# Cross-attention: the last quarter of V's projection as three products of parts, and a ring of nine probability tiles

## What is computed

```
q = x @ w_q                                   # 512 x 320
k = text @ w_k;  v = text @ w_v               # 1593 x 320, contraction over 512
out_text = softmax(q k^T / 4) v               # per head
out_ip   = softmax(q k_ip^T / 4 + mask) v_ip  # per head, 8 tokens, mask from boxes
y = (out_text + out_ip) @ w_out + b_out + x
```

## Time and profile before

| | |
|---|---|
| median of three runs | 1859.44 us (1856.71 to 1864.67) |
| profiled execution | 1859.6 us |
| its span | 1857.8 us, 42311 instructions |
| TensorE busy | 98% of the span |
| VectorE, ScalarE, GpSimd busy | 72%, 64%, 20% |
| chain that ended last | TensorE 94%, VectorE 4%, DMA 1%, issue 1% |
| mean granted TensorE clock | 0.992 |

### The profile page before, as it was taken

The page is one execution under the profiler, slowest core; times in us unless marked ns, Lnnn a source line. Parts: engine busy times, 40 slices in busy tenths (PEclk is TensorE's granted clock), DMA queues, the critical chain, the costliest instruction groups (busy, mean ns, idle before and its releaser), DMA issues.

```text
span 1857.8 us, 42311 instructions
## 1 busy us (share of the span) xinstructions
PE 1820.1 (98%) x17536; PEld 730.9 (39%) x17536; DVE 1336.7 (72%) x1705; ACT 1189.1 (64%) x2344; POOL 379.6 (20%) x475
## 2 busy tenths in 40 slices
PE   8999999999999999999999999999999999999997
PEld 3333343433344343443434434344334443344432
DVE  5878777787767867777777777767777777777861
ACT  1277666666666666666666666666666666666674
POOL 5112212212112211122211211122222212211000
PEclk9999999999999999999999999999999999999988
DMA  8556344353445444464443644436344453343300
GB/s 229 89 90 160 73 77 98 72 153 76 85 88 139 87 91 92 75 155 89 83 91 72 167 75 80 87 73 171 71 76 88 75 161 75 75 101 67 84 17 24
DMA packets 99761, 178.00 MB, mean 96 GB/s; under 512 B 42853, under 2 KB 71062, under 8 KB 95826
## 3 DMA queue, kind: packets, MB, share of 16 engines
q1 hardware_dynamic: 78578, 133.89, 37.3%
q0 software_dynamic: 18976, 40.10, 6.8%
q10 hardware_dynamic: 2016, 1.31, 0.2%
HBM read 117.57 MB, written 48.82 MB: 90 GB/s over the span
## 4 chain that ended last, share of the span: by engine, by line
PE 94%; DVE 4%; DMA 1%; issue 1%; ACT 0%; SPq 0%; POOLq 0%; POOL 0%; DVEq 0%
PE pv_bank L775 26%; PE max_bank L711 22%; PE work_bank L553 12%; PE work_bank L586 11%; PE exp_bank L759 10%; PE work_bank L609 3%; PE work_bank L564 3%; PE max_bank L722 2%; DVE tile_max L1045 2%; DVE tile_max L1038 1%; PE exp_bank L763 1%; PE work_bank L593 1%; PE work_bank L576 1%; PE work_bank L620 1%; DMA ctxt<-in_ctx_t 0%
## 5 line engine op out<-in xcount | busy, mean ns | idle before, releaser
L947 ACT ACTIVATE probs<-exp_bank 128x512 f32<-128x512 f32 x1896 | 995.7, 599 | 453.4 <-PE exp_bank L759 442.7
L1045 DVE TENSOR_REDUCE tile_max<-max_bank 128x2 f32<-128x1024 f32 x632 | 774.1, 1225 | 393.3 <-PE max_bank L711 388.5
L711 PE MATMUL max_bank<-k_stack,q_stack 48*128 48x512 f32 x1896 | 562.8, 466 | 14.4 <-DVE tile_max L1045 11.7
L775 PE MATMUL pv_bank<-probs,v_ones 128*17 128x512 f32 x3840 | 517.5, 603 | 0.1
L1047 DVE TENSOR_REDUCE tile_max<-max_bank 128x1 f32<-128x512 f32 x632 | 430.1, 680 | 0.0
L759 PE MATMUL exp_bank<-q_stack,k_stack 50*128 50x512 f32 x1896 | 411.5, 402 | 1.2 <-ACT probs L947 1.2
L711 PEld LDWEIGHTS max_bank<-k_stack,q_stack 48*128 48x128 f32 x1896 | 234.8, 185 | 411.1 <-issue 253.8
L553 PE MATMUL work_bank<-ctxt,wk 128*32 128x400 f32 x2528 | 253.5, 506 | 7.9 <-DMA wk<-in_w_k 5.6
L759 PEld LDWEIGHTS exp_bank<-q_stack,k_stack 50*128 50x128 f32 x1896 | 238.1, 188 | 41.5 <-ACT probs L947 31.0
L586 PE MATMUL work_bank<-wv,ctxt 128*32 128x320 f32 x3040 | 246.9, 434 | 0.0
L1246 POOL DMA_DIRECT2D sums<-o_sum x39 | 27.4, 703 | 666.0 <-ACT o_sum L887 666.0
(11 more groups left out here) (119 smaller groups left out, 858.5 us busy)
## 6 DMA issues: line engine op xcount, KB each, us to landing
k_stack<-scratch_k SPq DMA_DIRECT2D x234, 200.0 KB, 6.7
scratch_k<-k_parts SPq DMA_DIRECT2D x80, 400.0 KB, 4.7
ctxt<-in_ctx_t POOLq DMA_DIRECT2D x28, 800.0 KB, 11.3
q_stack<-scratch_q SPq DMA_DIRECT2D x240, 64.0 KB, 2.3
scratch_q<-q_parts SPq DMA_DIRECT2D x80, 128.0 KB, 5.6
r_wide<-scratch_r POOLq DMA_DIRECT2D x39, 256.0 KB, 5.2
xres<-in_x SPq DMA_DIRECT2D x8, 640.0 KB, 6.7
out<-xres SPq DMA_DIRECT2D x32, 160.0 KB, 2.0
```

What stands on the lines that cost most here:

```text
L711: nc.tensor.matmul(round_place(n, r)[:, k, :], exact(q_stack[stack, slot, c, t * 128:(t + 1) * 128]), exact(k_stack[stack, slot, c, chunk ...
L775: last = nc.tensor.matmul(pv_bank[h * 32:h * 32 + VW, :], v_ones[:, v_slot(b, kt), head * VW:(head + 1) * VW], p, start=(kt == 0), stop=(k ...
L947: nc.scalar.activation(dst, exp_place(group_no, at), ACT.Exp, scale=SCALE).then_inc(probs_ready, 1)
L1045: nc.vector.reduce_max(flat[:, at:at + 2], place[:, 0:2, :], AX.X).then_inc(max_taken, 1)
```

## The change

The last of V's four contraction quarters is no longer a float32 product in strips. GpSimd writes a high and a low part (float32r) of the last 128 rows of the context, `ctx_parts`, once a batch, and of `w_v`, `wv_parts`, once; TensorE adds high x high, high x low and low x high, each one matmul of 128 x 128 weights and 320 columns over the whole array. In batch 0 this holds only for V tiles below `V_EARLY` (those computed ahead for batch 1). V 12, the tail, and the prologue stay as they are. GpSimd's new work stands behind `split_q` and `load_x` of group 2. In group 2, V 0 and the first half of K 5 change places, and both wait for the context. The probabilities now stand in a ring of nine single tiles that runs through full and tail tiles of all groups; ScalarE waits for the PV of the tile that stood in the place nine tiles before.

```diff
-PROB_RING = 3
+PROB_RING = 9
@@ work_plan
-        put(2, ("V", 0), 4, (4, 1), (5, 3))
-        put(2, ("K", 5, 0), 4, (6, 1), (7, 1), (8, 2))
+        put(2, ("K", 5, 0), 4, (4, 1), (5, 3))
+        put(2, ("V", 0), 4, (6, 1), (7, 1), (8, 2))
@@ tiles
+        ctx_parts = sb("ctx_parts", [128, PARTS, KEYS])
+        wv_parts = sb("wv_parts", [128, PARTS, D])
-        probs = sb("probs", [128, PROB_RING, GH, S])
-        probs_tail = sb("probs_tail", [128, GH // 2, S])
+        probs = sb("probs", [128, PROB_RING, S])
+        ctx_high = sem("ctx_high")
+        ctx_split = sem("ctx_split")
+        def probs_place(n, at):
+
+            return probs[:, (n * EXPS + at) % PROB_RING, :]
+
+        def pv_of(tile):
+
+            n, at = tile // EXPS, tile % EXPS
+            return n * KT + at // GH + 1
@@ TensorE
-            def v_piece(t, ct_range, place=work_bank):
+            def v_piece(t, ct_range, place=work_bank, parts=False):
                 for ct in ct_range:
-                    if t < FULL:
+                    if parts and ct == CT - 1 and t < FULL:
+
+                        for a, b in ((0, 0), (0, 1), (1, 0)):
+                            last = nc.tensor.matmul(place[:, 0:D], exact(ctx_parts[:, a, t * 128:(t + 1) * 128]),
+                                                    exact(wv_parts[:, b, :]), start=False, stop=(a == 1))
+                    elif t < FULL:
                         for at, rows in strips(128):
...
                 if kind == "K":
+                    if piece[1] == 5 and begins(turn):
+                        pe.wait_ge(ctx_next_loaded, (b + 1) * CT * 16)
...
-                    v_piece(piece[1], range(turn[0], turn[1]))
+                    parts = not first or piece[1] < V_EARLY
+                    if parts and ends(turn) and piece[1] == 0:
+                        pe.wait_ge(ctx_split, b + 1)
+                    v_piece(piece[1], range(turn[0], turn[1]), work_bank, parts)
@@ ScalarE, exp_tile
-                kt, j = at // GH, at % GH
-                if j == 0:
-
-                    if kt == FULL:
-                        done = group_no * KT
-                    elif kt >= PROB_RING:
-                        done = group_no * KT + kt - PROB_RING + 1
-                    else:
-                        done = (group_no - 1) * KT + kt + FULL - PROB_RING + 1
-                    if done > 0:
-                        act.wait_ge(pv_done, done)
-                dst = probs[:, kt % PROB_RING, HEADS_IN_TURN[j], :] if kt < FULL else probs_tail[:, j, :]
+
+                tile = group_no * EXPS + at - PROB_RING
+                if tile >= 0 and (tile == 0 or pv_of(tile) != pv_of(tile - 1)):
+                    act.wait_ge(pv_done, pv_of(tile))
+                dst = probs_place(group_no, at)
@@ GpSimd
+            def split(parts, whole, n):
+                nc.gpsimd.tensor_tensor(exact(parts[:, 0, :]), whole, zero[:, :].to_broadcast(whole.shape), ALU.add).then_inc(ctx_high, 1)
+                pool.wait_ge(ctx_high, n)
+                return nc.gpsimd.tensor_tensor(exact(parts[:, 1, :]), whole, parts[:, 0, :], ALU.subtract)
+
+            def split_ctx(b):
+                if b == 1:
+                    split(wv_parts, wv[:, CT - 1, :], 1)
+                pool.wait_ge(ctx_next_loaded, b * CT * 16)
+                split(ctx_parts, ctxt[:, CT - 1, :], b + 1).then_inc(ctx_split, 1)
+
...
                             if piece == ("Q", 4) and not last:
                                 load_x(b + 1)
+                                split_ctx(b + 1)
```

More of the change, by code:

```diff
@@ L269, in cross_attention @@
         p_turned = s_ip[:, :, :].rearrange("p q n -> p (q n)").rearrange("p (j t n) -> p j t n", j=TURNED, t=QT)
-        early = probs[:, :, :, :].rearrange("p a h n -> p (a h n)")
+        early = probs[:, :, :].rearrange("p a n -> p (a n)")
         wk_ip = early[:, 0:CT * D].rearrange("p (c n) -> p c n", c=CT)
@@ L773, in pv_tile @@
                     head = g * GH + h
-                    p = probs[:, kt % PROB_RING, h, :] if kt < FULL else probs_tail[:, side_of(h)[1], :]
+                    p = probs_place(group_no, kt * GH + (HEADS_IN_TURN.index(h) if kt < FULL else side_of(h)[1]))
                     last = nc.tensor.matmul(pv_bank[h * 32:h * 32 + VW, :],
```

## The result

The changed kernel takes 1892.84 us (median of six runs, 1888.17 to 1895.10) beside 1859.25 for the kernel before; the ratio is 1.0174, 95% interval 1.0153 to 1.0196. That is slower by some 32 us and outside the predicted range. The profiled execution took 1888.76 us.

A forecast was written before the change was run, and what follows sets the result against it. TensorE, busy 98% of the span, was taken to bound the kernel. 1859.6 us plus 7.6 for 84 V tiles at +0.09, with GpSimd's parts, exchange and ring at 0, gave 1867.2 us, 0.4% slower; range 1860 to 1874.

The forecast's parts named there:

- TensorE's chain, the count and the price of a tile: V's last quarter: TensorE's time moves the end one for one; 84 tiles at +0.09 us, +7.6 us.
- The entry of 0.11 us: From PV's strips into the whole-array products: the array empties, 0.11 us a tile.
- the first weights of 0.11: At a tile's first whole-array product: a load of weights that nothing hides, 0.11 us.
- the excess: A 512-column matmul's 0.23 us is 0.017 above 512/2.4 ns; taken as proportional to columns, 0.144 us for 320.
- Rival 1: Strips to whole-array products without emptying, first weights loaded ahead: -10.9 us, 1848.7 us; 8%.
- Rival 2: Whole-array products' weights not loaded under the one before: +0.31 us a tile, +26, 1886 us; 5%.
- Exchange and ring: K 5 and V 0 exchanged: 0, within 0.5 us; nine probability tiles in turn: 0, at most 1 us.
- GpSimd's parts ... Cost: 0: GpSimd's split of the context, 6.4 us once a batch, fits its queue and is ready in time: 0.
- the bound of 13 us: Upper bound for GpSimd's context split, twice 6.4 us, should it slow down beside VectorE; 3 us of slack left.
- All other engines have slack: Steady part: only TensorE's own time moves the end, one for one; the other engines have slack.
- The clock: All stretches that hold the changed tiles: 1.00, the 2.4 GHz level.
- rival 3: GpSimd's parts or scaling come too late: 0.5 to 2 us in each of 7 batches, 1871 to 1881 us; 4%.

The follow-up runs named there:

- no_split: Changed kernel with GpSimd writing the context's parts only once, for batch 1, and an 8-column addition in later batches; 1866.91 us, 1.0050.
- neither: Changed kernel with all of V's contraction in strips and the context's parts written only once; 1862.69 us, 1.0011.
- low_later: Changed kernel, complete, with GpSimd's second operation on the context waiting until VectorE has added the mask; 1868.45 us, 1.0051.
- mask_later: Changed kernel, complete, with VectorE's image-prompt mask addition, maximum and subtraction in visits 5, 6, 7 instead of 3, 5, 6; 1864.37 us, 1.0047.
- four_pieces: Changed kernel, complete, with each of GpSimd's two operations on the context cut into four of 400 columns; 1865.18 us, 1.0043.
- early_split: Changed kernel, complete, with GpSimd's split of the context right behind its loads, at the end of group 1; 1865.46 us, 1.0040.
- split_only: Changed kernel with all of V's contraction in strips as before; GpSimd still writes the parts, which nobody reads; 1876.73 us, 1.0104.
- exchange_undone: Changed kernel with K 5 and V 0 back at their old visits; 1894.55 us, 1.0192.
- one_input: Changed kernel with VectorE's mask addition replaced by a multiplication of the same columns with 1.0, no mask added; 1883.01 us, one run.

## Why the prediction was wrong

**TensorE's chain, the count and the price of a tile: right.** 84 tiles at +0.09 us, +7.6 us. `no_split` less `neither` is 0.0039, 7.2 us, which their intervals leave open by some 5 us; the four mended complete kernels (`low_later`, `mask_later`, `four_pieces`, `early_split`) lie at 1.0040 to 1.0051, 7.4 to 9.5 us. The firmer proof is the trace: 0.99 and 0.64 us where 0.98 and 0.64 were worked out. The entry of 0.11 us (0.12), the first weights of 0.11 and the 0.144 a product (0.143 to 0.149) stand; whether the excess is exactly proportional, 0.144, or fixed, 0.150, hardly matters and leans to the former. Rival 1, no emptying, is out by the 0.99 from PV to the first product. Rival 2, weights in the open, had as its sign that products follow each other by 0.25: only the first interval of a tile is that long, as it holds the first weights, and the others are not.

**Exchange and ring: right**, 1.0011 with an interval that holds 1. ScalarE's waits for PV before an exponential, which the kernel before did not have, come to 0.7 us in two places.

**"GpSimd's parts ... Cost: 0": wrong, and with it all that failed.** The step asked whether GpSimd's queue had room and whether the parts would be there in time. It had and they were: the operations took 2.89 and 3.61 us where 2.8 and 3.6 were worked out, from 624.8 to 631.4, and V 0 did not wait. It allowed that GpSimd might slow down beside VectorE (the bound of 13 us), but not that VectorE might be held, and did not ask what VectorE does in those 6.4 us. The row to read was L1074's in the timeline of VectorE, the mask addition of visit 3 in the trace before:

```profile
619.11 0.82 DVE L1074 TENSOR_TENSOR s_ip<-s_ip,mask 128x640 f32<-128x640 f32 x1
```

It lies in the middle of the interval 615.9 to 622.3 that I had worked out for GpSimd. What was put at 0 was in fact 3.2 us more of VectorE's time in each of six batches, 2.2 us of TensorE's, and the clock's fall behind it. In the kernel before, GpSimd's longest operation on SBUF in the loop took some 1.3 us, so a meeting could hold VectorE little; the new ones are 2.2 and 2.8 times as long. The rule on the shared port, cited above, speaks against this very step, and it was not weighed.

**"All other engines have slack": wrong as used.** VectorE is idle for 28% of the span, but it must deliver the maxima every visit, 2.5 us or so. Of 3.2 us more in one visit some 1 us was hidden and 2.2 were not, whatever the average.

**The clock: not in the sum.** The prediction had the clock at 1.00 in all stretches that hold the changed tiles and took it to stay there. A stall of 2.35 us was followed by 3.4 us at 1.2 GHz, and K 5's turn took 3.92 instead of 2.22: 1.7 us, some three quarters of the stall's length.

The sum in the profiled executions: products 7.6, stalls 13.4 (25.1 less 11.7), six more falls of the clock at 1.7 make 10.2, together 31.2 against a span longer by 29.1. The rest, -2.1, I have not settled. The last batch spends less time at 1.2 GHz than before (18.8 against 29.4 us by the clock's record). That has its sign, but at half the clock it could be worth up to 5.3 us, so the sum closes only within some 3 us.

Of rival 3 ("GpSimd's queue becomes late", 1871 to 1881) only the place was right. It looked for the damage at those who wait for GpSimd's result, and the one who suffered waits for nothing of it.

By ratios: split alone (`split_only` less `neither`) 0.0093, 17 us; split beside whole products (the changed kernel less `no_split`) 0.0124, 23 us. The difference of 6 us is smaller than what the four intervals leave open (some 9 us, an estimate from their widths), so it is not shown that the two parts do anything but add. The number of falls of the clock behind stalls, three and six in the two profiles, would account for 5 us of it; why a stall of the same length is followed by a fall in one case and not in another was not tested.

## What to carry to other kernels

Work that is given to an idle GpSimd has to be laid against VectorE's timeline instruction by instruction: in these traces an elementwise operation there with SBUF in and out waited for the rest of the GpSimd instruction that was running (4.02 instead of 0.81 us), so cut long ones or order them by a wait (one wait took back some 23 us here). A cheaper count of columns on TensorE has to be laid against the change of shape that it adds: here 0.22 us for emptying and bare weights against 0.13 us of columns saved. And where the clock falls behind a wait of the bounding engine, the wait costs more than its length: here 2.35 us and 1.7 more.

## What the runs showed of the hardware that was not expected

- VectorE's elementwise operations on SBUF, with two tensor inputs or with one and a scalar, stood for the rest of a running GpSimd instruction (4.02 and 3.69 us, against 0.81 and 0.48 alone); a reduction of the same tile did not (0.81). GpSimd stood for VectorE in turn: 1.62 instead of 1.04 us.
- A whole-array float32r matmul of 320 columns, its weights loaded each time, follows the one before after 0.143 to 0.149 us, one of 512 in halves after 0.23: about 0.45 ns a column, 8 to 10% over the 0.417 ns of 2.4 GHz. Float32 in strips shows less: PV's four passes of 512 columns take 0.87 us, 0.425 ns a column.
- TensorE standing for 2.2 to 2.5 us in a stretch that is otherwise busy was followed by 3.4 us at 1.2 GHz in all six cases of the changed kernel, in all six of `exchange_undone` (once 6.8 us) and in three of six of `split_only`; standing for 1.9 to 2.0 us in `one_input`, in four of six.
